# Taking the reciprocal square roots of all norms on another engine, and moving one scatter in POOL's queue

## What is computed

```python
x = x + window_attention(ln_c(x))        # 8 heads, 8x8 windows with stride 4, out of 128 channels
t = tokens(x); t = t + moe0(ln_t(t))     # 8 experts, all computed, top 2 weighted
x = x + conv_block(ln_c(x))              # conv1 -> GN -> 9x9 depthwise + channel taps -> GN -> relu
                                         # -> conv2 -> GN -> relu
t = tokens(x); t = t + moe1(ln_t(t))     # 16 experts, only the chosen 2 per token
# ln: (v - mean) / sqrt(var + eps);   GN: (v - mean) * rsqrt(var + eps) * gamma + beta
```

## Time and profile before

| what | us |
|---|---|
| median of 3 runs (lowest, highest) | 875.82 (875.78, 880.25) |
| the profiled execution | 873.5 |
| its span (first to last instruction) | 871.7 |
| busy in the span: PE, DVE, ACT, POOL | 580.0, 367.1, 313.7, 384.4 |

### The profile page before, as it was taken

The page is one execution under the profiler, slowest core; times in us unless marked ns, Lnnn a source line. Parts: engine busy times, 40 slices in busy tenths (PEclk is TensorE's granted clock), DMA queues, the critical chain, the costliest instruction groups (busy, mean ns, idle before and its releaser), DMA issues.

```text
span 871.7 us, 15991 instructions
## 1 busy us (share of the span) xinstructions
PE 580.0 (67%) x5352; PEld 477.9 (55%) x5353; DVE 367.1 (42%) x1109; ACT 313.7 (36%) x746; POOL 384.4 (44%) x425
## 2 busy tenths in 40 slices
PE   0569999774799999959779422431599840799300
PEld 0357777562587777737458311331599830799300
DVE  5757777347205001160265751540255410355622
ACT  1648888621335444420412210200255410455200
POOL 5369999321636666622000275067100077000374
PEclk9969999957789999969779655565699965899755
DMA  7423333233223433930000012011133322232322
GB/s 291 113 59 88 88 86 87 83 169 115 101 81 116 145 145 122 281 94 0 1 0 1 15 52 66 0 52 55 49 87 96 88 64 54 74 91 82 107 81 60
DMA packets 81257, 74.97 MB, mean 86 GB/s; under 512 B 9068, under 2 KB 74820, under 8 KB 80684
## 3 DMA queue, kind: packets, MB, share of 16 engines
q1 hardware_dynamic: 76588, 64.72, 23.4%
q0 software_dynamic: 4608, 9.45, 3.7%
HBM read 50.92 MB, written 23.63 MB: 86 GB/s over the span
## 4 chain that ended last, share of the span: by engine, by line
PE 48%; POOL 15%; another core or an unknown queue 12%; DVE 10%; issue 8%; ACT 4%; DMA 2%; SPq 0%; POOLq 0%; DVEq 0%; ACTq 0%
PE bank L719 10%; PE bank L680 7%; PE bank L664 7%; PE bank L786 7%; PE bank L730 5%; POOL gathered_or_att L485 4%; POOL padded_or_w L476 4%; POOL gathered_or_att L546 4%; PE bank L226 3%; POOL gathered_or_att L494 2%; PE bank L642 2%; DVE ln_stats L991 2%; DVE normed L1010 1%; PE bank L710 1%
## 5 line engine op out<-in xcount | busy, mean ns | idle before, releaser
L546 POOL DMA_INDIRECT gathered_or_att<-sorted_y,slot x72 | 68.5, 951 | 178.4 <-DMA sorted_y<-padded_or_w 157.1
L534 POOL DMA_INDIRECT sorted_x<-normed,slot x72 | 69.7, 967 | 146.4 <-DVE slot L1178 125.1
L522 POOL TENSOR_TENSOR padded_or_w<-padded_or_w,gathered_or_att 128x384 f32<-128x384 f32 x96 | 95.7, 1002 | 73.5 <-ACT padded_or_w L896 49.5
L1207 DVE TENSOR_TENSOR att_or_moe<-att_or_moe,bank 128x256 f32<-128x256 f32 x104 | 43.7, 421 | 140.1 <-ACT att_or_moe L910 66.2
L680 PEld LDWEIGHTS bank<-moe_or_conv,padded_or_w 128*128 128x128 f32 x576 | 80.6, 197 | 34.0 <-issue 8.9
L896 ACT ACTIVATE padded_or_w<-bank,moe_b 128x384 f32<-128x384 f32 x96 | 55.6, 581 | 90.2 <-PE bank L664 90.1
L719 PE MATMUL bank<-att_or_moe,chan_major 128*128 128x128 f32 x416 | 61.2, 295 | 39.1 <-issue 28.1
L680 PE MATMUL bank<-moe_or_conv,padded_or_w 128*128 128x128 f32 x576 | 83.1, 283 | 4.1 <-POOL padded_or_w L522 4.1
L664 PE MATMUL bank<-chan_major,moe_or_conv 128*128 128x384 f32 x192 | 83.2, 520 | 1.9 <-ACT padded_or_w L896 1.9
L910 ACT ACTIVATE att_or_moe<-bank 128x256 f32<-128x256 f32 x104 | 40.0, 385 | 114.7 <-PE bank L719 63.8
L730 PE MATMUL bank<-w,att_or_moe 128*128 x416 | 66.4, 284 | 19.4 <-ACT padded_or_w L915 15.4
(11 more groups left out here) (167 smaller groups left out, 1079.1 us busy)
## 6 DMA issues: line engine op xcount, KB each, us to landing
gathered_or_att<-combine SPq DMA_DIRECT2D x24, 768.0 KB, 4.0
padded_or_w<-windows SPq DMA_DIRECT2D x192, 48.0 KB, 2.0
sorted_x<-zeros SPq DMA_DIRECT2D x26, 256.0 KB, 3.6
padded_or_w<-sorted_x SPq DMA_DIRECT2D x26, 256.0 KB
sorted_y<-padded_or_w SPq DMA_DIRECT2D x26, 256.0 KB, 2.4
padded_or_w<-in_moe_w SPq DMA_DIRECT2D x1, 4096.0 KB, 12.3
residual<-in_x_tok SPq DMA_DIRECT2D x2, 1152.0 KB, 6.4
out<-residual SPq DMA_DIRECT2D x12, 192.0 KB
```

What stands on the lines that cost most here:

```text
L522: nc.gpsimd.tensor_tensor(HB[n % DRING], HB[n % DRING], GB_[k % 3][:, n % 4, :], ALU.mult).then_inc(S("gated"), 1)
L534: nc.gpsimd.indirect_dma_start(xs_dram[b], bass.IndirectOffsetOnAxis(ap=POS[b][:, k, t:t + 1], axis=0), TN[b][:, t, :], None).then_inc(S(f ...
L546: nc.gpsimd.indirect_dma_start(G[k][:, t, :], None, ys_dram[b], bass.IndirectOffsetOnAxis(ap=POS[b][:, k, t:t + 1], axis=0)).then_inc(S(f" ...
```

## The change

The square root on ACT and the reciprocal on DVE become one instruction on POOL: the variance column(s) to the power of -0.5, taken elementwise against a constant tile `MHALF`. DVE waits for `ln_rstd`/`gn_rstd` where it waited for `ln_std`/`gn_std`. POOL therefore takes part in every phase that has a norm, at the place that the phase has in the order. Two pieces of its work move: the building of `toeplitz` goes behind the power of `LNA` 0, and the scatter of image 0 goes from `RS` 0 to behind the power of `LR` 1 1. The memset L527 now stands behind the powers of `XL` 1 and `XM` 0.

```diff
+        MHALF = sb("minus_half", [P, TT])
...
+            nc.gpsimd.memset(MHALF[:, :], -0.5).then_inc(S("half_set"), 1)
...
+            def ln_rstd(ph):
+                pool.wait_ge(S("ln_var"), ln_no(ph))
+                nc.gpsimd.tensor_tensor(LNV[:, 5, :], LNV[:, 3, :], MHALF[:, :], ALU.pow).then_inc(S("ln_rstd"), 1)
+            def gn_rstd(ph):
+                gv, n = GVB[ph[1]], gn_no(ph)
+                pool.wait_ge(S("gn_var"), n + 1)
+                nc.gpsimd.tensor_tensor(gv[:, 9:10], gv[:, 5:6], MHALF[:, 0:1], ALU.pow).then_inc(S("gn_rstd"), 1)
+            def lna(b):
+                ln_rstd(("LNA", b))
+                if b == 0:
+                    toeplitz()
             def residual(l, b):
+                ln_rstd(("LR", l, b))
                 if l == 0:
                     add_normed(("LR", 0, b), b)
+                elif b == 1:
+                    scatter(0)
+            def conv_norm(b):
+                ln_rstd(("XL", b))
+                add_normed(("XL", b), b)
+            def conv1(b):
+                pad(b)
+                gn_rstd(("XC", b))
...
-            run(A=..., LR=residual, D=dense, XL=lambda b: add_normed(("XL", b), b), XC=pad, RS=scatter, F=gather)
+            run(LNA=lna, A=..., LR=residual, D=dense, XL=conv_norm, XC=conv1, XM=lambda b: gn_rstd(("XM", b)),
+                XU=lambda b: gn_rstd(("XU", b)), RS=lambda b: scatter(b) if b else None, F=gather)
...
-                nc.scalar.activation(LNV[:, 4, :], LNV[:, 3, :], ACT.Sqrt).then_inc(S("ln_std"), 1)
-                nc.scalar.activation(gv[:, 6:7], gv[:, 5:6], ACT.Sqrt).then_inc(S("gn_std"), 1)
...
-                dve.wait_ge(S("ln_std"), ln_no(ph))
+                dve.wait_ge(S("ln_rstd"), ln_no(ph))
-                link(nc.vector.reciprocal(LNV[:, 5, :], LNV[:, 4, :]))
...
-                dve.wait_ge(S("gn_std"), n + 1)
-                link(nc.vector.reciprocal(gv[:, 9:10], gv[:, 6:7]))
+                dve.wait_ge(S("gn_rstd"), n + 1)
```

More of the change, by code:

```diff
@@ L450, in _ @@
             pool.wait_ge(S("consts_in"), 64)
-            pool.wait_ge(S("small_in"), 16 * 7)
-            for a in range(KA):
-                for r in range(4):
-                    nc.gpsimd.tensor_tensor(TOEP[:, a * KX:(a + 1) * KX, 32 * r:32 * r + 32], I32.unsqueeze(1).broadcast_to([P, KX, 32]),
-                                            W2R[:, 4 * a - r + 3, :].unsqueeze(2).broadcast_to([P, KX, 32]), ALU.mult)
-            nc.gpsimd.tensor_scalar(BAND[:, :], DJ[:, 0:32], W1C[:, 1:2], None, ALU.mult).then_inc(S("band"), 1)
@@ L459, in _ @@
[L459 to L467, removed]
+            pool.wait_ge(S("half_set"), 1)
@@ new lines, in toeplitz @@
+            def toeplitz():
+                pool.wait_ge(S("small_in"), 16 * 7)
+                for a in range(KA):
+                    for r in range(4):
+                        nc.gpsimd.tensor_tensor(TOEP[:, a * KX:(a + 1) * KX, 32 * r:32 * r + 32], I32.unsqueeze(1).broadcast_to([P, KX, 32]),
+                                                W2R[:, 4 * a - r + 3, :].unsqueeze(2).broadcast_to([P, KX, 32]), ALU.mult)
+                nc.gpsimd.tensor_scalar(BAND[:, :], DJ[:, 0:32], W1C[:, 1:2], None, ALU.mult).then_inc(S("band"), 1)
+                for j in range(1, 7):
+                    nc.gpsimd.tensor_scalar(BND[:, :], DJ[:, 32 * j:32 * j + 32], W1C[:, j + 1:j + 2], None, ALU.mult).then_inc(S("band"), 1)
+                    pool.wait_ge(S("band"), 2 * j)
+                    nc.gpsimd.tensor_tensor(BAND[:, :], BAND[:, :], BND[:, :], ALU.add).then_inc(S("band"), 1)
+                    pool.wait_ge(S("band"), 2 * j + 1)
+                for r in range(4):
+                    blk = TOEP[32 * r:32 * r + 32, KX + KX // 2, 32 * r:32 * r + 32]
+                    nc.gpsimd.tensor_tensor(blk, blk, BAND[32 * r:32 * r + 32, :], ALU.add).then_inc(S("toeplitz"), 1)
+                    pool.wait_ge(S("toeplitz"), r + 1)
@@ L548, in gather @@
                                                      ).then_inc(S(f"gathered{gather_part(t)}"), 16)
-            run(A=lambda n: attend(att, n), LR=residual, D=dense, XL=lambda b: add_normed(("XL", b), b), XC=pad, RS=scatter, F=gather)
+            run(LNA=lna, A=lambda n: attend(att, n), LR=residual, D=dense, XL=conv_norm, XC=conv1, XM=lambda b: gn_rstd(("XM", b)),
+                XU=lambda b: gn_rstd(("XU", b)), RS=lambda b: scatter(b) if b else None, F=gather)
         @block.tensor
@@ L827, in lna @@
             def lna(b):
-                sqrt_of(("LNA", b))
                 if b == 0:
@@ L928, in conv_norm, with gn_coef @@
             def conv_norm(b):
-                sqrt_of(("XL", b))
                 evac(("XL", b), QY[b])
-            def gn_sqrt(ph):
-                gv, n = GVB[ph[1]], gn_no(ph)
-                act.wait_ge(S("gn_var"), n + 1)
-                nc.scalar.activation(gv[:, 6:7], gv[:, 5:6], ACT.Sqrt).then_inc(S("gn_std"), 1)
-                act.wait_ge(S("gn_coef"), n + 1)
+            def gn_coef(ph):
+                gv = GVB[ph[1]]
+                act.wait_ge(S("gn_coef"), gn_no(ph) + 1)
                 return {"bias": gv[:, 8:9], "scale": gv[:, 7:8]}
@@ L946, in conv1 @@
                     nc.scalar.activation(HC[b][:, hh, :], banks[C1[b][hh]][:, 0:HALF], ACT.Identity, bias=C1B).then_inc(S("hc_ready"), 1)
-                norm = gn_sqrt(("XC", b))
+                norm = gn_coef(("XC", b))
                 act.wait_ge(S("pad_zero"), b + 1)
@@ L954, in conv_mid @@
             def conv_mid(b):
-                norm = gn_sqrt(("XM", b))
+                norm = gn_coef(("XM", b))
                 for hh in range(2):
@@ L968, in conv2 @@
                                          ACT.Identity, bias=C2B).then_inc(S("up_out"), 1)
-                nc.scalar.activation(QY[b][:, :], CM[b][:, :], ACT.Relu, **gn_sqrt(("XU", b))).then_inc(S("z3_ready"), 1)
+                nc.scalar.activation(QY[b][:, :], CM[b][:, :], ACT.Relu, **gn_coef(("XU", b))).then_inc(S("z3_ready"), 1)
             act.wait_ge(S("consts_in"), 64)
-            run(LNA=lna, A=lambda n: attend(att, n), LR=lambda l, b: sqrt_of(("LR", l, b)), RT=route_a, RC=logit_exp, D=dense, M=moe,
+            run(LNA=lna, A=lambda n: attend(att, n), RT=route_a, RC=logit_exp, D=dense, M=moe,
                 XL=conv_norm, XC=conv1, XM=conv_mid, XU=conv2)
```

2 lines of the change are left out of this document (removed).

## The result

The changed kernel takes 891.38 us against 877.10 before (medians of 4 runs each on one chip); the ratio is 1.0168, with a 95% interval of 1.0138 to 1.0199. The forecast was 873.7 with a range of 867 to 887: the time lies outside it.

The account below looks back on a forecast made before the run. The prediction saw no single bounding engine: PE, the busiest, works two thirds of the span, so time is a sum of stages. Terms summed to −2.1 us on 873.5; with 2.3 to the median, 873.7, range 867 to 887.

Parts of the forecast that it names:

- scatter leaves `XU` 1, `XZ` 1: `XU` 1 to `LR` 1 1 without image 0's stores falls from 14.81 to 12.48 us: −2.3 (0 to −2.3).
- norm `LR` 1 1 and routing, to the second scatter: Image 1's routing under the moved scatter: 0 (−6.1 to +13), and +0.1 for the layer norm's power.
- behind the second scatter: Image 0's experts, SP's loads and stores, `M` 1 and the gathers move with the second scatter, unchanged.
- the price of the power: One POOL power, in no profile row: 0.6 us for 18 columns, 0.3 for one; upper bound 2.2.
- a dear power: Rival, start and four layer norms: at 3 us for 18 columns +14.4, so 888.1 us; chance 0.15.
- The start: `LNA` 0 and 1: clean first steps, paid back by slower normalizing and late tap matrices; −0.1 (−0.8 to +3.1).
- The norms on the path: Layer norms `LR` 0 0, `LR` 0 1, `XL` 0, `LR` 1 1: +0.1 each, +0.4 in all (−0.9 to +6.8).
- Group norms: `XC` 0, `XM` 0, `XC` 1, `XM` 1, `XU` 1: 0.35 us instead of 0.44, −0.5 in all (−0.8 to 0).
- The memset: A POOL memset of 0.75 us beside DVE's last three small instructions of `XM` 0: +0.4 (0 to 0.75).
- two scatters in a row: Rival: image 1's routing takes under 46.2 us, POOL issues 72 stores in one go; 870.0 us, chance 0.25.
- stage at its old length: Likeliest case: `LR` 1 1 to the second scatter stays at 52.3 us under the moved scatter; chance 0.38.
- the drag: Other engines work slowly while POOL issues indirect transfers, more so the longer it lasts; expected until 51.3 us after `LR` 1 1's mark.

Follow-up runs that it names:

- group_norms_only: Changed kernel with the layer norms back on ACT's square root and DVE's reciprocal; group norm powers, later tap matrices and moved scatter stay: 874.99 us, 0.9984.
- move_only: Kernel before with only image 0's scatter moved behind the small statistics of `LR` 1 1, all norms and tap matrices as before: 870.90 us, 0.9942.
- powers_only: Changed kernel with image 0's scatter back at `RS` 0, and `XU` 1 and `LR` 1 1 keeping square root and reciprocal: 892.17 us, 1.0188.
- price_list: Changed kernel with twelve POOL instructions, products and powers of several shapes, added behind its last gather: ends at 852.96 us.
- matrices_only: Kernel before with only the tap matrices built later, behind the small statistics of `LNA` 0: 767.33 us, 0.9993.

## Why the prediction was wrong, step by step

| step | forecast, us | two profiles, us |
|---|---|---|
| start, up to `LR` 0 0 | −0.1 | +4.4 |
| norms `LR` 0 0, `LR` 0 1, `XL` 0 | +0.3 | +9.9 |
| `XC` 0 to `XU` 1 without the next row: group norms, memset | −0.1 | −0.7 |
| `LR` 1 0 to `XM` 1 | 0 | +3.1 |
| scatter leaves `XU` 1, `XZ` 1 | −2.3 | −3.6 |
| norm `LR` 1 1 and routing, to the second scatter | +0.1 | −1.6 |
| behind the second scatter | 0 | +4.8 |
| sum | −2.1 | +16.3 |

**The step that failed** is the price of the power: "I take 0.6 us for 18 columns, nearer to the lower end because the fixed part is paid once". It is 3.22, above even the upper bound of 2.2, which was a guess of eight plain instructions: no run shows what steps a power is made of. The reason given was upside down: the fixed part is small (one column, fixed part included, takes 0.57 us), and the column part, for which the forecast took 1.5 ns or thirteen times that from plain instructions, is 160 ns. By the forecast's own slope, two at the start and four in the norms, 2.62 us more give +15.7; the rival "a dear power" had this, with 888.1 at 3 us and a chance of 0.15. Shown by group_norms_only and move_only (gone without the powers), powers_only (there without the move) and price_list.

**The start** was right in form: clean first steps, 9.3 us of normalizing ("over 8"), POOL late with the matrices, and both powers on the path. matrices_only shows that its edit is worth about nothing. The ACT table load left the path; with a power of 3.2 us in its place this is no gain. The first power begins 0.18 us behind DVE's last small step (13.25) and takes 3.25 us, as the later ones do. The Trainium skill (GPSIMD Engine Reference, section 2.1) has about 6 us for the first call of a freshly loaded routine; at this place the trace shows nothing of it.

**The norms on the path.** 2.7 us each make 8.1 of the 9.9. The stretch `LR` 0 1 to `XL` 0 grew by 2.1 more than its norm: it takes 156.4 us in the profile before and 156.4 to 159.6 in those of all kernels without layer norm powers, 160.2 to 161.7 with them undoubled, so before happened to be at the low end. `LR` 1 0 and `XL` 1 were rightly called hidden, at this price; at twice the price `LR` 1 0 is not.

**Group norms.** Off by sign: +0.15 to +0.2 each. Too small to be seen in the sum. The memset cost nothing.

**`LR` 1 0 to `XM` 1.** No step of the forecast: a stretch of PE work at a lower granted clock (0.59 and 0.50 where the kernel before has 1.00 and 0.82). Its 3.1 us return in every kernel with all group norm powers; the cause of that is open.

**The scatter.** Leaving `XU` 1 gave 3.6 where 2.3 were forecast with "0 to −2.3" as bounds. The stage behind: the rival "two scatters in a row" came true, the forecast's own "stage at its old length" did not, and it was close, with the routing ready 1.3 us before POOL. It gave −4.3 without the norm's 2.7, for −6.1 (from the first store to the first of image 1 pass 47.3 us where 45.5 were taken), and 4.8 came back behind it, where 2.4 was taken and 4.7 thought of as the most. With `XU` 1 the scatter is worth −3.1 in the two profiles, near the forecast's −2.3, but in other pieces than the sum had. move_only has the same mechanism, with 4.1 of 9.5 us kept. That the drag might not be there at all was no case of the forecast; on a chip of the free kind the move costs 2%, and the whole change 5%.

**In sum** one term decided: 15.7 us of price, for a power that the sum had at 0.6 us. The clock's 3.1 us in `LR` 1 0 to `XM` 1 come on top, and the scatter gave about what was forecast.

## What to carry to other kernels

An operation that the trace doesn't show has no price until it is measured: a bound made from other operations of that engine was short by a third, and what is slow is the column, so a power for few columns is cheap and for 18 not. When work on a serial queue (here POOL's 36 stores of 1.26 us) is moved behind a mark, ask when the queue is needed next: all 72 stores then stand between the mark and the end, which costs nothing only where something else is slow anyway. Leaving a third of the stores at the old place kept the queue free in time, and was the fastest kernel on one kind of chip (0.9819) and no worse on the other (0.9990 to 1.0004).

## What the runs showed of the hardware

The power on POOL takes 0.57 us for 1 column, 0.77 for 2, 1.64 for 8, 3.21 for 18, 6.12 for 36, about the same on 32, 64 and 128 partitions; a product of 18 columns takes 0.23.

The slowness of the other engines while POOL issues indirect transfers is not the same on all chips. With the same program, packets and bytes the kernel before took 874 to 877 us on three occasions and 768 on three others; in the first 40 us of the second scatter five and a half or 24 tiles were done, and from its last store to the first gather passed 80 us (614.68 to 694.83) or 41 (589.65 to 630.20). The instructions themselves keep their length under it; what grows are pauses in front of them (DVE's routing steps, 0.45 us each, stand 1.40 us apart in the changed kernel, 0.49 without drag). Nothing that the traces show tells why.

PE's granted clock gave the same stretch of work 29.33 to 29.35 us in eleven profiles and 32.44 to 32.46 in eight, with nothing in between.
